# First convolution with one-hot tables laid out node number by node number, VectorE's order changed, weight loads moved ahead

## The chip, the cores and the metric

The kernel runs on one core of a Trainium2 chip. The metric is the device time of one execution in microseconds (us); the figure quoted is the median of the runs. The engines are TensorE (PE in the rows; PEld is its weight load), VectorE (DVE), ScalarE (ACT), GpSimd (POOL) and SyncE (SP). They work through their own instruction streams side by side and wait for one another on semaphores. A q behind an engine's name (DVEq, SPq) marks its instruction sequencer. "Window 300:1480" means from 300 to 1480 us after the start.

## The reference, cut to what matters

A graph with 12,500 nodes and 212,500 edges, sorted by the node that they end in. Three convolutions of one kind run first, then a layer norm, two layers of another kind and a last norm. Only the first convolution and the preparation ahead of it are touched.

```
def conv(h, W, b):
    m = jnp.concatenate([h[dst], h[src], edge_attr], axis=1) @ W + b
    return jax.ops.segment_sum(m, dst, num_segments=n_nodes)
h = jax.nn.relu(conv(x, W1, b1))
h = jax.nn.relu(conv(h, W2, b2))
return conv(h, W3, b3)
```

Since the sum over a node's edges commutes with the product by `W`, the kernel first sums the source nodes' rows and the edge attributes by node, and multiplies afterwards.

## The kernel before

**Tiling.** Edges stand in columns of 128 (one edge to a partition); 11 columns (`GC`) are a group, 8 groups (`TURN`) a turn, and 19 turns (`KT`) the whole. Groups alternate between two kinds, `KINDS = "EPEPEPEP"`. I call an E group and the P group behind it a quarter; there are 76 quarters.

- A **P** group fetches its source rows from HBM: GpSimd issues 11 indirect DMAs (`data<-h_parts,idx`, L913), two buffers deep.
- An **E** group fetches nothing. For each of its 11 columns ("steps" 0 to 10 below) a table of counts is made by matmuls, from `low_hot` (the low 7 bits of the source number as a one-hot row, the stationary operand) and `high_hot` (high bits and place): one of 66 columns into `p_end` (L1025), two of 506 into `p_count` (L1028). ScalarE casts `p_count` (L1152), and VectorE `p_end` in two halves (`evacuate_end`, L1366), into `adj`. A quarter later `adj` is the stationary operand of 98 matmuls against all node features `hs` (L1041, into `p_z`), 8 or 9 to each step, issued right behind the step's counts. ScalarE also sends `adj` to HBM for the later convolutions (L1161).

Both kinds sum the edge attributes, and P its rows too, by destination: 11 matmuls with `hot[:, par, j, :]` as the stationary operand (L928), `hot` being the one-hot table of the group's places, 11 blocks of 128 fp16 or bf16 numbers. `turn` (L935, L936) brings that sum into `p_node`, `finish` (L1326) adds it to `acc`, `scatter` (L1057) and `finish_dense` (L1378) do the same for `p_z`.

**What sets the order.** Each engine's stream is written out by hand in `conv_pass`; there is no scheduler. TensorE runs `dense` (11 steps; the E group's L928 behind step 1), then the P group's L928, then `scatter`. VectorE runs one `pair` (L1357, a `high_hot` table) to each step, with other work between pairs: `build_hot` (L1247) at steps 4 and 8, `rest_part` (L1278) at 3, 5, 7 and 9, `low_digits` (L1348, L1349, the next quarter's `low_hot`) at 9, `evacuate_end` and both `finish` at 6 and 2. TensorE's step m waits for pair m (`s_pair`) and for the cast of step m-2; pair m waits for the counts of step m-2, since `high_hot` has two buffers. `finish` and `finish_dense` read their base address from an SBUF table into a register (`value_load`; TENSOR_LOAD in the rows) where they need it.

**The preparation** (`prepare`) splits `x` into three bf16 parts (`xs`, `hs`), makes the tables (`chip.place`, `chip.lo`, `chip.code`), folds the weights of the two last layers (`WeightSteps`), and stores what later stages need. Layer 0's weights are loaded by SyncE behind the `hs` stores, layer 1's by GpSimd behind its iotas. Its last instruction is SyncE's wait for its stores (`s_kept`, `s_flags`, `s_parts`); all engines then meet, and the first convolution begins.

Of the kernel before, what the change touches and what calls it, by code (L numbers as in the profile page):

```python
# [25 lines left out]
P = 128  # L26
# [19 lines left out]
GC = 11  # L46
KINDS = "EPEPEPEP"
# [181 lines left out]
def prepare(chip, x_pad, src_cols, dst_pad, dst_cols, heads, col_ends, col_heads, firsts, slot_heads, flags, parts,  # L229
# [11 lines left out]
    with ExitStack() as ctx:  # L241
# [74 lines left out]
        def _(sp):  # L316
# [12 lines left out]
            steps[0].load(sp)  # L329
# [9 lines left out]
            for rows_of_it, tile in ((kept.ends, pna_ends), (kept.regs, pna_regs)):  # L339
                sp.dma_start(rows_of_it, tile[:, :, :]).then_inc(s_kept, 16)  # L340
            sp.dma_start(kept.quads, pna_quads[:, :]).then_inc(s_kept, 16)
            count = 48
            for layer, w in enumerate(ws):
                sp.wait_ge(steps[layer].s_done, 1)
                sp.wait_ge(steps[layer].s_one, 4)
                for rows_of_it, tile in zip(kept.weights[layer], w.tiles):
                    sp.dma_start(rows_of_it, tile.ap()).then_inc(s_kept, 16)
                    count += 16
            sp.wait_ge(s_kept, count)
# [4 lines left out]
        def _(pool):  # L354
            iota = lambda out, pattern, base, step: pool.iota(out, pattern, base=base, channel_multiplier=step,
                                                              allow_small_or_imprecise_dtypes=True)
            pool.memset(chip.ident[:, :], 0.0).then_inc(s_zero, 1)
            iota(chip.ramp[:, :], [[1, P]], 0, 0)
# [10 lines left out]
            for step in steps[1:]:  # L369
                step.load(pool)  # L370

        @block.vector
        def _(v):
# [10 lines left out]
            v.memset(chip.place[:, 0:2, :], -1.0)  # L384
            v.memset(chip.place[:, NGC + 2:, :], -1.0)
# [48 lines left out]
            in_group = chip.place[:, 2:NGC + 2, :].rearrange("p (h s) j -> p h s j", s=TURN)  # L434
# [6 lines left out]
            tables = [t[:, 1:NE + 1, :].rearrange("p (h s) j -> p h s j", s=NQ) for t in (chip.lo, chip.code)]  # L441
# [57 lines left out]
            v.tensor_copy(chip.cregs[:, 4, 1:], base[:, :])  # L499
            v.memset(chip.eregs[:, 2, 0:1], N)  # L500
# [41 lines left out]
        def _(act):  # L542
# [23 lines left out]
            for step in steps[1:]:  # L566
                step.scalar(nc, act, own)
# [99 lines left out]
def conv_pass(chip, layer, table, src_cols, ea_cols, W, bias, out_rows, counted, degree_rows=None):  # L667
# [29 lines left out]
    with ExitStack() as ctx:  # L697
# [8 lines left out]
        hot = sb("hot", [P, 2, GC, P], BF16)  # L706
        if first:
            low_hot = sb("low_hot", [P, 2, GC, P], F16)
            code = sb("code", [P, 2, GC])
            high_hot = sb("high_hot", [P, 2, BLOCKS * WIN], F16)  # L710
# [185 lines left out]
        def _(pool):  # L896
# [8 lines left out]

            further_windows_of(pool, further)
# [12 lines left out]
        def _(pe):  # L919
# [93 lines left out]
            def dense(k, q, count=True, between={}):  # L1013
                for i in range(GC):
                    m = q * GC + i
                    if count and first:
# [8 lines left out]
                        pe.matmul(p_end[:, b * (HI_B * WIN):(b + 1) * (HI_B * WIN)], low_hot[:, q % 2, i, :],  # L1025
                                  high_hot[:, m % 2, SPLIT:], start=True, stop=True)
                        for a in range(2):
                            mm = pe.matmul(p_count[:, m % 2, a, 0:BANK], low_hot[:, q % 2, i, :],  # L1028
# [211 lines left out]
        def _(v):  # L1240
# [3 lines left out]
            def build_hot(k, n):  # L1244
                places = chip.place[:, bass.ds(place_of(k, n), 1), :].rearrange("p a j -> p (a j)")
                ramp = chip.ramp16[:, :] if first else p_end[:, 0:P]
# [81 lines left out]
            def further(k, pos, m, x):  # L1328
# [6 lines left out]
                v.tensor_copy(near[:, :].unsqueeze(1), chip.place[:, bass.ds(k * TURN + (pos + 2), 1), :]).then_inc(s_near, 1)  # L1335
# [8 lines left out]
            def low_digits(k, q):  # L1344
                at = bass.ds(k * NQ + (q + 1), 1)
                gate(v)
                digits = chip.lo[:, at, :].rearrange("p a j -> p (a j)")
# [32 lines left out]
            def far_windows(k, q, m, x):  # L1380
# [6 lines left out]
                v.tensor_scalar(col(0).unsqueeze(1), chip.place[:, bass.ds(k * TURN + (POS_E[q] + 2), 1), :],  # L1387
# [4 lines left out]
                v.tensor_copy(col(5).unsqueeze(1), chip.lo[:, bass.ds(entry, 1), :])  # L1392
# [82 lines left out]
            if not first:  # L1475
                v.wait_ge(s_ramp, 1)
# [1042 lines left out]
```

## Time and profile before

| | us |
|---|---|
| median of 3 runs | 8308.83 (8302.76 to 8309.02) |
| profiled execution: its time | 8316.16 |
| profiled execution: span of the profile | 8314.4 |
| in it: preparation | 0 to 100.6 |
| first convolution, up to the end of its loop over edges | 100.6 to about 1480 |
| its matmuls over nodes | about 1480 to 1560 |
| all that follows | 1560 to 8314.4 |

Over the whole span TensorE is busy for 82%, GpSimd for 71%, VectorE for 53% and ScalarE for 28%. These are means over stages with different limits, so the prediction reads the preparation and the first convolution's loop by themselves. In that loop the granted TensorE clock is 1.00 throughout. The profiled execution is 7.3 us longer than the median.

### The profile page before, as it was taken

Reading aid. Unit: us, or ns where it says so; the run is one execution under the profiler, and the core shown is the slowest. Engines: PE = TensorE matmul, PEld = TensorE weight load, DVE = VectorE, ACT = ScalarE, POOL = GpSimd, SP = SyncE. Lnnn points to the kernel's source line nnn. Section 1 sums busy time; section 2 is a strip of 40 time slices with the busy share of each in tenths; the row PEclk is TensorE's granted clock in tenths of the full one; section 3 lists DMA queues with packets and bytes.
Section 4 is the critical chain, followed back from the end, with each engine's and each line's share of the span. In section 5 each row is a group of like instructions: output and inputs, shape, how many; then the busy total and the mean of one; then the engine's idle time right before and its main releaser. Section 6 shows DMA issues by size and latency. Waiting matters only on the chain. (4 is left out here: it accounts for less than half of the span.)

```text
span 8314.4 us, 168220 instructions
## 1 busy us (share of the span) xinstructions
PE 6837.9 (82%) x53896; PEld 5544.3 (67%) x53897; DVE 4427.7 (53%) x5884; ACT 2338.0 (28%) x3847; POOL 5877.8 (71%) x5876
## 2 busy tenths in 40 slices
PE   4999999888888799886788888788858888888885
PEld 3666666778888688885666666666656666566663
DVE  6777777522222222224566556566556656566665
ACT  3777777300000000002222222222242222222223
POOL 3888888177777677774777777777557777777773
PEclk9999999698888788987899889988878899898897
DMA  4655656377778777774222222222222222222222
GB/s 152 222 219 217 225 214 222 110 280 275 275 272 273 254 274 273 274 283 135 66 74 67 69 68 72 72 66 71 58 78 68 71 66 70 70 71 70 66 71 63
DMA packets 417038, 1226.32 MB, mean 147 GB/s; under 512 B 121988, under 2 KB 221694, under 8 KB 368304
## 3 DMA queue, kind: packets, MB, share of 16 engines
q1 hardware_dynamic: 216553, 744.06, 25.1%
q0 software_dynamic: 187232, 233.06, 12.9%
q10 hardware_dynamic: 13160, 248.08, 7.4%
q8 instruction: 44, 0.72, 0.0%
q14 instruction: 49, 0.40, 0.0%
HBM read 943.22 MB, written 281.51 MB: 147 GB/s over the span
## 5 line engine op out<-in xcount | busy, mean ns | idle before, releaser
L1913 POOL DMA_INDIRECT data<-q_rows,idx x3328 | 3163.8, 951 | 1145.3 <-issue 998.6
L913 POOL DMA_INDIRECT data<-h_parts,idx x2508 | 2676.0, 1067 | 1098.9 <-issue 1077.9
L1041 PE MATMUL p_z<-hs,adj 128*128 128x192 bf16 x22442 | 2115.6, 252 | 61.8 <-issue 61.7
L1041 PEld LDWEIGHTS p_z<-hs,adj 128*128 128x128 bf16 x22442 | 1934.2, 100 | 314.0 <-issue 106.1
L2045 ACT COPY back<-p_back 128x1024 f32<-128x1024 f32 x418 | 423.2, 1013 | 2385.1 <-PE p_back L1933 2385.1
L2115 DVE TENSOR_TENSOR_SCAN run<-reset,run,p_turn 128x1024 f32<-128x1024 bf16 x416 | 974.2, 2342 | 145.0 <-PE p_turn L1980 141.4
L1152 ACT CAST adj<-p_count 128x1012 bf16<-128x1012 f32 x836 | 918.7, 1105 | 334.6 <-PE p_count L1028 334.5
L573 DVE TENSOR_TENSOR hot<-p_ramp,ends 128x2048 f32<-128x2048 f32 x416 | 949.7, 2283 | 0.6 <-issue 0.5
L1939 PE MATMUL part<-hot,t 128*128 128x128 f32 x6688 | 908.7, 295 | 45.5 <-issue 45.5
L1939 PEld LDWEIGHTS part<-hot,t 128*128 128x128 f32 x6688 | 878.6, 212 | 46.1 <-issue 46.1
L1944 PE MATMUL part<-hot,back 128*128 128x128 f32 x6688 | 815.1, 275 | 0.0
L2082 DVE TENSOR_TENSOR t<-data,p_feat 128x512 f32<-128x512 f32 x416 | 285.7, 687 | 978.7 <-DMA data<-q_rows,idx 719.9
L1933 PEld LDWEIGHTS p_back<-ident,run 128*128 128x128 f32 x3344 | 428.4, 157 | 557.3 <-issue 557.3
L1944 PEld LDWEIGHTS part<-hot,back 128*128 128x128 f32 x6688 | 779.8, 192 | 0.0
L1933 PE MATMUL p_back<-ident,run 128*128 128x128 f32 x3344 | 511.6, 303 | 244.1 <-DVE run L2115 244.0
L1925 PE MATMUL p_feat<-w_edge_feat,feat 128*128 128x512 f32 x832 | 482.2, 664 | 208.1 <-DVE acc L2143 171.3
L1301 DVE TENSOR_REDUCE zs<-p_z 128x64 f32<-128x192 f32 x229 | 80.7, 352 | 964.9 <-PE p_z L1041 964.9
L1226 ACT CAST idx<-src_near 128x11 int32 x228 | 45.7, 201 | 1816.6 <-DMA data<-h_parts,idx 1738.3
L1028 PE MATMUL p_count<-high_hot,low_hot 128*128 128x506 f16 x1672 | 495.7, 377 | 0.0
L1357 DVE TENSOR_SCALAR high_hot<-iota,code 128x1078 f16<-128x1078 f16 x838 | 420.8, 510 | 51.7 <-PE p_count L1028 44.0
L1980 PE MATMUL p_turn<-ident,t 128*128 128x128 f32 x3328 | 435.7, 274 | 0.0
L928 PE MATMUL p_part<-data,hot 128*128 128x192 bf16 (+1 forms) x2508 | 281.9, 264 | 175.0 <-DMA data<-h_parts,idx 174.8
(314 smaller groups left out, 6388.5 us busy)
## 6 DMA issues: line engine op xcount, KB each, us to landing
adj<-counted SPq DMA_DIRECT2D x304, 1568.0 KB
counted<-adj ACTq DMA_DIRECT2D x76, 3136.0 KB
reset<-flags SPq DMA_DIRECT2D x208, 512.0 KB
data<-q_rows,idx POOLq DMA_INDIRECT x3328
data<-h_parts,idx POOLq DMA_INDIRECT x2508
feat<-in_ea_blocks SPq DMA_DIRECT2D x208, 128.0 KB
ea<-in_ea_cols SPq DMA_DIRECT2D x154, 88.0 KB, 1.9
rden<-node_rows SPq DMA_DIRECT2D x50, 256.0 KB
```

The lines of the kernel that those rows point to most:

```text
L573: return v.tensor_tensor(hot.rearrange("p t j n -> p (t j) n"), chip.p_ramp[:, :].unsqueeze(1).broadcast_to([P, 2 * G, P]), places.unsquee ...
L913: pool.indirect_dma_start(out=data[:, p % HELD, j, 0:PARTS], out_offset=None, in_=table[:, :], in_offset=bass.IndirectOffsetOnAxis(ap=idx[ ...
L1028: mm = pe.matmul(p_count[:, m % 2, a, 0:BANK], low_hot[:, q % 2, i, :], high_hot[:, m % 2, a * BANK:(a + 1) * BANK], start=True, stop=True)
L1041: mm = pe.matmul(p_z[:, 0:PARTS], adj[:, (q + LAG) % 2, hi, :], hs[:, hi, :], start=(hi == 0), stop=(hi == BLOCKS - 1))
L1152: nc.scalar.copy(to, p_count[:, m % 2, :, 0:BANK].rearrange("p a (h w) -> p a h w", w=WIN))\
L1913: pool.indirect_dma_start(out=data[:, r, j, :], out_offset=None, in_=q_rows[:, :], in_offset=bass.IndirectOffsetOnAxis(ap=idx[:, r, j:j + ...
L1925: pe.matmul(p_feat[:, r % 2, :], feat[:, r, :], w.edge[:, :, :].rearrange("p j f -> p (j f)"), start=True, stop=True).then_inc(s_feat, 1)
L1933: b = pe.transpose(p_back[:, j * P:(j + 1) * P], run[:, par, j * P:(j + 1) * P], chip.ident[:, :])
L1939: pe.matmul(part[:, x, 0, :], t3[:, slot, j, 1:3, :].rearrange("p b f -> p (b f)"), hot[:, par, 0, j, :], start=(j == 0), stop=(j == G - 1))
L1944: m = pe.matmul(part[:, x, 1, :], back[:, j, :], hot[:, par, 1, j, :], start=(j == 0), stop=(j == G - 1))
L1980: m = pe.transpose(p_turn[:, j * P:(j + 1) * P], t3[:, r, j, 0:2, :].rearrange("p b f -> p (b f)"), chip.ident[:, :])
L2115: v.tensor_tensor_scan(run[:, r % 2, :], reset[:, r, :], p_turn[:, :], run[:, (r + 1) % 2, GE - 1:GE], ALU.add, ALU.max).then_inc(s_run, 1)
```

## The change

**Tables.** In the first convolution a table is no longer 11 blocks of 128 numbers but 128 blocks of 12 (`GW`), a node number's 11 columns and one of padding side by side. The number ramp against which it is compared is written out in that form (`wide_ramp`, 1536 numbers, by GpSimd at the start of the convolution); `chip.place` and `chip.lo` get rows of 12. TensorE takes a column's table as stationary operand with 12 numbers from one element to the next.

**VectorE.** `low_digits` goes from step 9 to behind step 10. The bases of the two `finish` of a quarter come packed from one `value_load` ahead of the first pair (`both_begins`, table `chip.begins`); `finish_dense` uses the one already read, but for the first quarter of a turn.

**Preparation.** GpSimd loads both layers' weights ahead of its iotas, ScalarE makes both layers' weights before `start`, and SyncE stores them before it stores `flags` and the `kept` tables.

```diff
@@ prepare, SyncE
-            steps[0].load(sp)
             sp.wait_ge(s_wins, 1)
...
-            sp.wait_ge(s_start, 1)
-            sp.dma_start(flags.rearrange("(p e) -> p e", p=P), start[:, :]).then_inc(s_flags, 16)
-            sp.wait_ge(s_pna, 1)
...
             for layer, w in enumerate(ws):
                 sp.wait_ge(steps[layer].s_done, 1)
...
+            sp.wait_ge(s_start, 1)
+            sp.dma_start(flags.rearrange("(p e) -> p e", p=P), start[:, :]).then_inc(s_flags, 16)
+            sp.wait_ge(s_pna, 1)
...
@@ prepare, GpSimd
             pool.memset(chip.ident[:, :], 0.0).then_inc(s_zero, 1)
+            for step in steps:
+                step.load(pool)
...
-            for step in steps[1:]:
-                step.load(pool)
@@ prepare, VectorE and ScalarE
+            halves = chip.begins[:, :].bitcast(I16)
+            v.memset(halves[:, 0:1], N)
+            v.tensor_copy(halves[:, 1:NGC + 1], base[:, :])
...
-            steps[0].scalar(nc, act, own)
+            for step in steps:
+                step.scalar(nc, act, own)
             act.wait_ge(s_begin, 1)
@@ conv_pass
+            wide_ramp = sb("wide_ramp", [P, P, GW], F16)
+            wide_hot = sb("wide_hot", [P, 2, P, GW], BF16)
+            low_hot = sb("low_hot", [P, 2, P, GW], F16)
...
+            if first:
+                pool.iota(wide_ramp[:, :, :], [[1, P], [0, GW]], base=0, channel_multiplier=0,
+                          allow_small_or_imprecise_dtypes=True).then_inc(s_ramp, 1)
...
-                    mm = pe.matmul(p_part[:, columns(pos)], hot[:, par, j, :],
+                    mm = pe.matmul(p_part[:, columns(pos)], wide_hot[:, par, :, j] if first else hot[:, par, j, :],
...
-                        pe.matmul(p_end[:, b * (HI_B * WIN):(b + 1) * (HI_B * WIN)], low_hot[:, q % 2, i, :],
+                        pe.matmul(p_end[:, b * (HI_B * WIN):(b + 1) * (HI_B * WIN)], low_hot[:, q % 2, :, i],
...
+                if first:
+                    return v.tensor_tensor(wide_hot[:, n % 2], wide_ramp[:, :, :],
+                                           chip.place[:, bass.ds(place_of(k, n), 1), :].broadcast_to([P, P, GW]), ALU.is_equal)
...
-                v.tensor_tensor(low_hot[:, q % 2], chip.ramp16[:, :].unsqueeze(1).broadcast_to([P, GC, P]),
-                                digits.unsqueeze(2).broadcast_to([P, GC, P]), ALU.is_equal)
+                v.tensor_tensor(low_hot[:, q % 2], wide_ramp[:, :, :], chip.lo[:, at, :].broadcast_to([P, P, GW]),
+                                ALU.is_equal)
...
+            def both_begins(k, pos):
+
+                two = v.value_load(chip.begins[0:1, bass.ds(k * (TURN // 2) + pos // 2, 1)], min_val=0,
+                                   max_val=(N << 16) + N)
+                low = v.snap((two & 0xffff).with_bounds(min_val=0, max_val=N))
+                return low, v.snap((two >> 16).with_bounds(min_val=0, max_val=N))
...
+                    before, begins[pos] = both_begins(k, pos)
+                    for i in range(2, GC):
+                        pair(k, q, i)
...
+                        if i == GC - 1:
+                            low_digits(k, q + 1)
```

**Place A: VectorE, behind the pair of step 6.** `p_end` is the first half's counts, `cregs` the table of bases, `high_hot` at the end the pair of step 7. Before:

```order
L1366 CAST adj<-p_end 128x6x6x11
L1316 ISA
L1316 TENSOR_LOAD cregs
L1316 ISA x2
L1326 ISA
L1326 TENSOR_TENSOR acc<-acc,p_node 49x128
L1370 ISA
L1370 TENSOR_SCALAR to_window<-ramp,slots 128x128
L1357 TENSOR_SCALAR high_hot<-iota_2,code 128x1078
```

With the change:

```order
L1379 CAST adj<-p_end 128x6x6x11
L1340 ISA
L1340 TENSOR_TENSOR acc<-acc,p_node 49x128
L1383 REGISTER_ALU
L1383 TENSOR_SCALAR to_window<-ramp,slots 128x128
L1370 TENSOR_SCALAR high_hot<-iota_2,code 128x1078
```

The register load has gone from between the cast and the sum; the next pair follows with nothing else between.

**Place B: VectorE, from the pair of step 9 on.** `low_hot` is the next quarter's table; the `high_hot` rows are the pairs of steps 9 and 10 and the next quarter's 0. Before:

```order
L1357 TENSOR_SCALAR high_hot<-iota_2,code 128x1078
L1276 REGISTER_ALU
L1278 TENSOR_TENSOR dense_ea<-ea,dense_ea 128x11x16
L1348 ISA
L1348 COPY code<-code 128x11
L1349 REGISTER_ALU
L1349 TENSOR_TENSOR low_hot<-ramp_2,lo 128x1408
L1356 REGISTER_ALU
L1357 TENSOR_SCALAR high_hot<-iota_2,code 128x1078
L1356 REGISTER_ALU
L1357 TENSOR_SCALAR high_hot<-iota_2,code 128x1078
```

With the change:

```order
L1370 TENSOR_SCALAR high_hot<-iota_2,code 128x1078
L1290 REGISTER_ALU
L1292 TENSOR_TENSOR dense_ea<-ea,dense_ea 128x11x16
L1369 REGISTER_ALU
L1370 TENSOR_SCALAR high_hot<-iota_2,code 128x1078
L1361 ISA
L1361 COPY code<-code 128x11
L1362 ISA
L1362 TENSOR_TENSOR low_hot<-wide_ramp,lo 128x1536
L1369 REGISTER_ALU
L1370 TENSOR_SCALAR high_hot<-iota_2,code 128x1078
```

The pair of step 10 now stands ahead of the table, which has 1536 elements instead of 1408.

**Place C: GpSimd, start of the preparation.** `own_place` is what VectorE's first instruction on the parts of `x` stands behind (`s_place`). Before:

```order
L357 MEMSET ident 128x128
L355 ISA
L355 IOTA ramp 128x128
L355 IOTA shifts 128x100
L355 IOTA near_shifts 128x32
L355 IOTA slot_w 128x1
L355 IOTA slot_w 128x11
L355 IOTA own_place 128x8
```

With the change:

```order
L357 MEMSET ident 128x128
L171 DMA wp_3<-in_L_gnn_W_pre 64x192
...
L171 DMA wo_3<-in_L_gnn_W_post 64x3x64 x5
L355 ISA
L355 IOTA ramp 128x128
...
L355 IOTA own_place 128x8
```

Thirty DMA issues, 15 for each layer, now stand between the memset and the iotas.

## Rows read from the trace of the kernel before

**Rows 1.** Busy time by stretch: length, PE, PEld, DVE, ACT, POOL, clock, DMA, GB/s.

```profile
500.00:1000.00 500.00, 456.60 (x4440) 340.46 (x4439) 378.36 (x781) 363.20 (x475) 404.12 (x308) 1.00 0.60 219
```

**Rows 2.** Groups by line and form, window 300:1480: count, busy us, mean ns, idle before.

```profile
L913 POOL DMA_INDIRECT data<-h_parts,idx x723 | 952.4, 1317 | 225.7 <-issue 225.7
...
L1247 DVE TENSOR_TENSOR hot<-ramp,place 128x1408 bf16<-128x1408 f16 x132 | 212.6, 1610 | 0.0
...
L1349 DVE TENSOR_TENSOR low_hot<-ramp,lo 128x1408 f16<-128x1408 f16 x66 | 106.6, 1615 | 0.0
...
L1278 DVE TENSOR_TENSOR ea<-ea,data 128x176 f32<-128x176 f32 x65 | 22.3, 343 | 18.9 <-ACT data L1173 18.9
...
L936 PEld LDWEIGHTS p_node<-ident,by_place 128*113 128x113 f32 x132 | 18.2, 178 | 0.0
```

**Rows 3.** Longest wait of TensorE, window 300:1480: total us, times, longest.

```profile
PE p_end L1025 <- DVE high_hot L1357: 74.9, 99, 0.9
```

**Rows 4.** Timeline, one quarter, TensorE at steps 6 to 10: start, length, instruction.

```profile
716.29 0.19 PE L1025 MATMUL p_end<-high_hot,low_hot 128*128 128x66 f16 x1 [0.20 <-DVE adj L1366]
...
718.08 0.19 PE L1025 MATMUL p_end<-high_hot,low_hot 128*128 128x66 f16 x1 [0.43 <-ACT adj L1152]
...
719.28 0.19 PE L1025 MATMUL p_end<-high_hot,low_hot 128*128 128x66 f16 x1
...
720.69 0.19 PE L1025 MATMUL p_end<-high_hot,low_hot 128*128 128x66 f16 x1
...
722.96 0.19 PE L1025 MATMUL p_end<-high_hot,low_hot 128*128 128x66 f16 x1 [0.91 <-DVE high_hot L1357]
```

**Rows 5.** Timeline, the same quarter, VectorE.

```profile
715.47 0.57 DVE L1366 CAST adj<-p_end 128x396 bf16<-128x396 f32 x1 [0.69 <-PE p_count L1028]
...
716.92 0.28 DVE L1326 TENSOR_TENSOR acc<-acc,p_node 49x128 f32 x1 [0.88 <-issue]
...
717.44 0.50 DVE L1357 TENSOR_SCALAR high_hot<-iota,code 128x1078 f16<-128x1078 f16 x1
...
720.79 1.61 DVE L1349 TENSOR_TENSOR low_hot<-ramp,lo 128x1408 f16<-128x1408 f16 x1
...
722.32 0.90 DVE L1357 TENSOR_SCALAR high_hot<-iota,code 128x1078 f16<-128x1078 f16 x2
```

**Rows 6.** Timeline, the same quarter: two gathers, and short matmuls.

```profile
708.28 0.95 POOL L913 DMA_INDIRECT data<-h_parts,idx  x1 [0.38 <-issue]
...
709.18 0.19 PE L1025 MATMUL p_end<-high_hot,low_hot 128*128 128x66 f16 x1
...
709.21 0.59 PE L1028 MATMUL p_count<-high_hot,low_hot 128*128 128x506 f16 x2
...
710.38 0.44 PE L928 MATMUL p_part<-dense_ea,hot 128*128 128x49 bf16 x11
...
712.07 2.30 POOL L913 DMA_INDIRECT data<-h_parts,idx  x1 [0.30 <-issue]
```

**Rows 7.** Timeline of the preparation: weight issues, VectorE on `x`, SyncE's stores.

```profile
3.22 0.76 POOL L170 DMA_DIRECT2D wp<-in_L_gnn_W_pre  x1
...
8.32 3.61 POOL L170 DMA_DIRECT2D wo<-in_L_gnn_W_post  x6
...
8.43 1.49 DVE L398 TENSOR_TENSOR xs<-xs,hs 128x1280 f32<-128x1280 f32 x1 [4.93 <-ACT hs L551]
...
30.19 0.22 DVE L411 CAST identb<-ident 128x128 bf16<-128x128 f32 x1
...
70.44 0.34 SPq L340 DMA_DIRECT2D kept_ends<-pna_ends  x1
...
79.12 0.60 SPq L347 DMA_DIRECT2D kept_w<-w_beta  x1
```

**Rows 8.** DMA busy tenths and GB/s, window 60:105, 40 slices of 1.125 us.

```profile
DMA  0063000000998907999099993420000000000710
GB/s 0 7 257 121 0 15 0 0 0 0 440 364 281 350 1 266 219 11 8 0 16 16 11 22 14 35 53 0 0 0 0 0 0 0 0 0 4 169 38 4
```

More of the change, by code:

```diff
@@ L46 @@
 GC = 11
+GW = 12
 KINDS = "EPEPEPEP"
@@ L440, in _ @@
             v.wait_ge(s_src, 16)
-            tables = [t[:, 1:NE + 1, :].rearrange("p (h s) j -> p h s j", s=NQ) for t in (chip.lo, chip.code)]
+            tables = [t[:, 1:NE + 1, 0:GC].rearrange("p (h s) j -> p h s j", s=NQ) for t in (chip.lo, chip.code)]
             then(v.tensor_scalar(digit[:, 0], dense(src), 7, None, ALU.arith_shift_right))
@@ L705, in conv_pass @@
         by_place = sb("by_place", [P, KC])
-        hot = sb("hot", [P, 2, GC, P], BF16)
+        if not first:
+            hot = sb("hot", [P, 2, GC, P], BF16)
         if first:
-            low_hot = sb("low_hot", [P, 2, GC, P], F16)
+            wide_ramp = sb("wide_ramp", [P, P, GW], F16)
+            wide_hot = sb("wide_hot", [P, 2, P, GW], BF16)
+            low_hot = sb("low_hot", [P, 2, P, GW], F16)
             code = sb("code", [P, 2, GC])
@@ L1244, in build_hot @@
             def build_hot(k, n):
-                places = chip.place[:, bass.ds(place_of(k, n), 1), :].rearrange("p a j -> p (a j)")
-                ramp = chip.ramp16[:, :] if first else p_end[:, 0:P]
+                if first:
+                    return v.tensor_tensor(wide_hot[:, n % 2], wide_ramp[:, :, :],
+                                           chip.place[:, bass.ds(place_of(k, n), 1), :].broadcast_to([P, P, GW]), ALU.is_equal)
+                places = chip.place[:, bass.ds(place_of(k, n), 1), 0:GC].rearrange("p a j -> p (a j)")
+                ramp = p_end[:, 0:P]
                 return v.tensor_tensor(hot[:, n % 2], ramp.unsqueeze(1).broadcast_to([P, GC, P]),
@@ L1474, in _ @@
             v.memset(scratch[:, 27:28], 0.0).then_inc(s_by_sum, 1)
-            if not first:
-                v.wait_ge(s_ramp, 1)
+            v.wait_ge(s_ramp, 1)
             for n in range(1 if first else 2):
@@ L1488, in _, with first_turn @@
             far_turns(v, far_windows)
-            with v.Fori(0, KT) as k:
+            def both_begins(k, pos):
[3 more added lines that the diff above has]
+                return low, v.snap((two >> 16).with_bounds(min_val=0, max_val=N))
+            def first_turn(k):
+                begins = {}
@@ L1490, in _ @@
                 for pos in range(TURN):
                     if pos in POS_P:
+                        q = POS_E.index(pos - 1)
+                        dense_begin = begins[pos - 3] if pos - 3 in begins else dense_begin_of(k, q)
+                        sum_z(k, q)
+                        sum_places(k, pos)
+                        finish_dense(k, q, k * H + (nth[pos] + 1 + BEFORE), dense_begin)
+                        continue
+                    q = POS_E.index(pos)
+                    before, begins[pos] = both_begins(k, pos)
@@ new lines, in first_turn @@
+                    for i in range(2, GC):
+                        pair(k, q, i)
+                        if i == 2:
+                            finish(k, pos - 1, before)
+                        if i in (3, 5):
+                            rest_part(k, nth[pos] + 1, (i - 3) // 2)
+                        if i in (4, 8):
+                            table_free(k, nth[pos] + (1 if i == 4 else 2))
+                            build_hot(k, nth[pos] + (1 if i == 4 else 2)).then_inc(s_hot, 1)
+                        if i == 6:
+                            evacuate_end(k, q, 0)
+                        if i == 6:
+                            finish(k, pos, begins[pos])
+                            place_slots(k, q)
+                        if i in (7, 9):
+                            rest_part(k, nth[pos] + 2, (i - 7) // 2)
+                        if i == GC - 1:
+                            low_digits(k, q + 1)
@@ L1492, in _ @@
+                    for i in (0, 1):
+                        pair(k, q + 1, i)
+                    evacuate_end(k, q, 1)
+            with v.Fori(0, KT) as k:
+                if first:
+                    first_turn(k)
+                for pos in (() if first else range(TURN)):
+                    if pos in POS_P:
                         dense_begin = {q: dense_begin_of(k, q) for q in done_with(pos)}
-                        if pos == POS_P[-1] and not first:
+                        if pos == POS_P[-1]:
```

61 lines of the change are left out of this document (19 added, 42 removed).

## The prediction

> **What bounds the kernel now.** I read the stages first. The change touches the preparation (100.6 us) and the loop over edges of the first convolution (about 1345 us after its start-up); the 6750 us behind them keep their instructions. In the loop no engine is the plain bound: TensorE is busy for 457 of 500 us, GpSimd for 404, VectorE for 378, ScalarE for 363, at a granted clock of 1.00, the upper level of 2.4 GHz [rows 1]. The table of low digits is built once a quarter, 66 times in 1180 us [rows 2]: a quarter takes 17.88 us, and there are 76.
>
> Next, who makes TensorE wait. Its largest wait is for VectorE's `high_hot`: 74.9 us in 66 quarters, 1.13 us each [rows 3]. The timeline of one quarter shows where. A step that nothing disturbs takes 719.28 - 718.08 = 1.20 us [rows 4]. Step 6 to 7 takes 1.79, so 0.59 is lost; step 8 to 9 takes 1.41, 0.21 lost; step 9 to 10 takes 2.27, 1.07 lost. VectorE's rows say why [rows 5]. Ahead of step 7 the half-cast ends at 716.04, the sum after it starts only at 716.92 (0.88 us "issue", the register load), and the pair runs 717.44 to 717.94; the matmul follows at 718.08. The row there names ScalarE, but the pair is what came last. Ahead of step 10, `low_hot` runs 720.79 to 722.40 and the pair behind it starts at 722.32. Step 9's pair stands behind a `hot` table in the same way. Sum: 1.87 us a quarter. Step 6 waits for the half-cast itself, which stays.
>
> GpSimd deserves a look of its own. All its idle time between gathers is "issue", 0.31 us each [rows 2]: busy plus idle is 1178 of 1180 us. A gather takes 0.95 us when left alone and 2.30 when it meets a table [rows 6]. Eleven undisturbed ones need 11 x (0.95 + 0.31) = 13.9 us, so 4.0 us a quarter go to collisions with three tables of 1.61 us (83% of their width).
>
> **The change, part by part.**
>
> *Tables in a shorter time.* Two rows give VectorE's rate: 1408 elements in 1.610 us and 176 in 0.343 [rows 2], hence 1.03 ns an element and 0.16 us fixed. At that rate 1536 elements need 1.74 us; at two elements a cycle, since ramp, places and result are all 16 bits wide and contiguous in the inner dimension, 0.95 us. No row shows a two-input 16-bit instruction with contiguous operands, so these are both ends. I take 0.95: `high_hot`, 16-bit and contiguous, does 1078 elements in 0.50 us [rows 5], well under one per cycle's time. With it step 9 loses nothing.
>
> *Order.* `low_hot` behind step 10's pair lets that pair go 1.6 us earlier, and step 10 starts on time. The table is then wanted only after 98 matmuls' tail, the P group's 11 matmuls and the scatter, over 2 us later. What is queued behind it is the pairs 0 and 1 of the next quarter and the second half-cast. One packed register load a quarter stands where VectorE has slack, ahead of the pair of step 2; the one between the half-cast and the pair of step 7 is gone, and with it the 0.88 us. Its sum, `finish`, moves earlier with it, and nobody else is late for it. So all 1.87 us should go: 76 x 1.87 = 142 us. What is late next is step 6's half-cast, unchanged.
>
> *Weight loads with 24 bytes between elements: a cost.* Every load of `low_hot` (3 a step) and `wide_hot` (11 a group) now picks single 16-bit numbers. No row shows such a load. Near end: contiguous 16-bit loads keep pace with 49-column matmuls, 11 in 0.44 us, or (0.44 - 0.19) / 10 = 0.025 us each [rows 6]. Far end: fp32 loads of 113 columns, in pairs, 18.2 us of cover for 66 pairs at 178 ns each, follow each other after 0.276 - 0.178 = 0.098 us [rows 2], or 0.111 for 128. A load is hidden behind the matmul ahead of it. At length L what sticks out is: behind the 66-column matmul, which lasts 0.03 (709.18 to 709.21 [rows 6]), L - 0.027, eleven times; in the E group's sum L - 0.025, eleven times; behind a 192-column matmul (192 / 2.4 GHz = 0.080) L - 0.08, eleven times; behind a 242-column one L - 0.10, eleven times. With L = 0.111 that is 11 x 0.21 = 2.3 us a quarter; with 0.025 nothing. I take twice the contiguous time, 0.051, nearer the row of the same type and form: 11 x (0.024 + 0.026) = 0.55, say 0.57 us a quarter with rounding, 43 us in all.
>
> Two statements of the Trainium skill pull apart here. "TensorE: Matmul & The Clock Gate", section "Weight-path perf modes", gives fast weight load's read pattern as four chunks of 32 columns, "packed or strided"; by that alone the load stays as it is and the whole comes to 8146. "SBUF - State Buffer" (Door 1, the note on cachelines) says that reads lose their rate when each goes to another 16-byte line, as they would at 24 bytes. No run so far shows either.
>
> *GpSimd.* Its collisions shrink with the tables: 83% of 3 x 0.95 = 2.4 us, so 16.2 us a quarter, under the 16.6 forecast for TensorE. The Trainium skill ("SBUF - State Buffer", Who interferes with whom) infers that `tensor_tensor` does not hold up descriptor generation; the trace disagrees, with 2.30 us against 0.95 [rows 6].
>
> *Preparation.* GpSimd needs 8.32 + 3.61 - 3.22 = 8.7 us to issue 15 loads [rows 7]; thirty in front of the iotas end at about 18.4, so VectorE's work on `x` begins near 20 and not at 8.43. It was waiting for pieces of `x` then and will not be now: ten instructions, one each 1.45 us, bring it to 34.5, where it had been at 30.2 [rows 7]. The rest of its stream follows 4.3 us later, plus 0.5 for new small instructions, so `kept_ends` goes out at 75.2, not 70.44. Against this stands the tail. SyncE's last issue ends at 79.7 [rows 7], the next stage starts at 100.6, and DMA stays busy at 11 to 53 GB/s until about 91.5 [rows 8], with the weight stores as the last in the queue. These now go out between about 46 and 62 us, under VectorE's work (the cover; without it they cost what they cost now). The 836 KB of `kept_ends` took some 3.5 us at 280 to 440 GB/s [rows 8]: stage end near 80 instead of 100.6. Should the tail belong to whatever is stored last, 76.2 + 20.9 = 97.1. I take 19 us, ends 3.5 and 21.
>
> *Start of the convolution.* `wide_ramp` is some 1.5 us on GpSimd, beside VectorE's memsets of several us; the first gathers are wanted 30 us later. Two tables ahead of the loop save 2 x 0.66 = 1.3 us.
>
> **Sum.** 142 - 43 + 19 + 1 = 119 us. 8316.2 (the profiled execution's time) - 119 = 8197; that execution was 7.3 above the median, so 8190.
>
> **The rivals.**
>
> *The strided load is as quick as before.* For it: the same instruction form. Then 8316.2 - 7.3 - 142 - 20 = 8147; should GpSimd at 16.2 us a quarter be the bound, 76 x 1.68 = 128 us and 8161.
>
> *The tables take 1.74 us,* or GpSimd or a later wait takes over. Step 9 keeps its 0.21 and 0.13 more, and the next quarter's first steps lose some 0.3: gain 1.2 - 0.57 = 0.65 us, 49 + 20 us, 8240. Against it: all three operands meet what `high_hot` meets.
>
> *Slower: TensorE becomes bound by its weight loads.* Place: the 44 loads a quarter named above. With L = 0.111 the cost is 2.3 us against 1.87 gained: 76 x 0.41 = 31 us lost, 20 won back, 8320, no change. From L = 0.113 on it is over 0.2% slower; at 0.15 it is 11 x (0.123 + 0.125 + 0.07 + 0.05) = 4.0 us, 2.2 a quarter, 164 - 20 = 144 us, 8453. For it: four chunks are read at once, each from another place at each element. Against it: the fp32 row moves twice the bytes and still does a column in 0.87 ns.
>
> *The change does not do what it says*: the moved table and the gone register load are plain in the instruction order, so only the preparation's tail could stay (8205); it is inside the forecast.
>
> **How the numbers follow.** Forecast, L from 0.035 to 0.075: 0.38, 8190 (8160 to 8240). Quick load: 0.25, 8147 to 8161. Long tables or another bound: 0.12, 8240. L from 0.075 to 0.10: 0.07, 8240 to 8290. L from 0.10 to 0.113, no change: 0.06. Slower: 0.12. Faster 0.82, same 0.06, slower 0.12; 0.2% (17 us) is about what a measurement of this kernel can tell from no change. The range 8135 to 8300 leaves out the slower case and the upper part of no change.
>
> **What would show each step.** In the changed kernel's profile: `wide_hot` and `low_hot` at 0.95 us; steps 7, 9 and 10 at 1.20 us plus the load; the 11 matmuls of 49 columns in 0.44 us (quick), near 0.7 (forecast) or over 1.3 (slower); a quarter of 16.6 us; gathers with a mean near 1.17 us (0.95 plus 2.4 / 11); the first convolution starting near 81 us. The forecast is wrong if those 11 matmuls take over 1.3 us, if ScalarE's casts turn out to pace the steps, or if the stage start stays at 97 or later.

## The result and the profile after

| | us |
|---|---|
| before, median (same chip) | 8305.8 (8298.6 to 8309.0) |
| after, median | 8208.1 (8207.5 to 8211.6) |
| ratio | 0.988, 95% interval 0.987 to 0.990 |
| after, profiled execution (span) | 8208.1 (8206.4) |

The change takes 98 us away. 8190 was forecast, in a range of 8135 to 8300. By the barriers between the stages, in the two profiled executions: preparation 100.0 us before, 79.5 after; first convolution 1543.5 and 1471.2. The stages behind them, whose code is the same, were 15 us shorter in the later execution. About half of that is the 7 us by which the profiled execution of before lay above its median; the other 8 us have no cause that a run shows. What the change did is therefore read from the two stages alone: 20.5 + 72.3 us.

Of the changed kernel, the busy time in the stretch of [rows 1]:

```profile
500.00:1000.00 500.00, 494.37 (x4701) 407.20 (x4699) 345.32 (x827) 386.30 (x502) 329.74 (x324) 1.00 0.64 233
```

TensorE was busy for 457 of 500 us and is for 494 now: it bounds the loop. Its groups and VectorE's and GpSimd's, window 300:1380, against [rows 2]:

```profile
L924 POOL DMA_INDIRECT data<-h_parts,idx x703 | 719.7, 1024 | 363.3 <-issue 194.7 <-PE p_part L939 168.5
...
L1039 PEld LDWEIGHTS p_count<-high_hot,low_hot 128*128 128x128 f16 x1404 | 147.9, 157 | 0.0
...
L1257 DVE TENSOR_TENSOR wide_hot<-wide_ramp,place 128x1536 bf16<-128x1536 f16 x128 | 121.6, 950 | 0.0
...
L1362 DVE TENSOR_TENSOR low_hot<-wide_ramp,lo 128x1536 f16<-128x1536 f16 x63 | 60.0, 952 | 0.0
```

The tables take 0.95 us instead of 1.61. A gather takes 1.02 us in the mean instead of 1.32, and 168.5 us of GpSimd's idle time now are waits for TensorE, where all of it had been "issue". The wait of [rows 3] is gone; the only one left of its kind, same window:

```profile
PE p_end L1036 <- DVE adj L1379: 8.8, 32, 0.3
```

Against [rows 4, 6], TensorE in one quarter of the changed kernel, steps 1 and 2 and 6 to 10:

```profile
692.26 0.78 PE L939 MATMUL p_part<-dense_ea,wide_hot 128*128 128x49 bf16 x11
...
692.88 0.22 PE L1036 MATMUL p_end<-high_hot,low_hot 128*128 128x66 f16 x1
...
698.72 0.22 PE L1036 MATMUL p_end<-high_hot,low_hot 128*128 128x66 f16 x1 [0.21 <-DVE adj L1379]
...
699.98 0.19 PE L1036 MATMUL p_end<-high_hot,low_hot 128*128 128x66 f16 x1
...
701.21 0.19 PE L1036 MATMUL p_end<-high_hot,low_hot 128*128 128x66 f16 x1
...
702.45 0.19 PE L1036 MATMUL p_end<-high_hot,low_hot 128*128 128x66 f16 x1
...
703.68 0.19 PE L1036 MATMUL p_end<-high_hot,low_hot 128*128 128x66 f16 x1
```

Step 7 follows 1.26 us after step 6, where it had been 1.79; step 9 after 1.24 (1.41) and step 10 after 1.23 (2.27). But the undisturbed step was 1.20 and is 1.24, and eleven 49-column matmuls take 0.78 us where they took 0.44: they start 0.059 us apart, not 0.026. Two amounts of opposite sign, then, and the experiments are there to part them. The clearest view is the mean time from a step's first matmul to the next step's, worked out from all quarters between 300 and 1250 us of each trace that have no record missing. The column names the step that it begins with, 10 holds the P group too, and the last one is the mean length of a quarter in the same stretch. Labels are those of the experiments below.

| kernel | 0 | 1 | 2 | 3 | 4 | 5 | 6 | 7 | 8 | 9 | 10 | quarter |
|---|---|---|---|---|---|---|---|---|---|---|---|---|
| before | 1.36 | 1.49 | 1.20 | 1.20 | 1.65 | 1.54 | 1.79 | 1.20 | 1.41 | 2.27 | 2.81 | 17.91 |
| after | 1.44 | 1.86 | 1.26 | 1.23 | 1.68 | 1.65 | 1.26 | 1.24 | 1.24 | 1.23 | 2.85 | 16.94 |
| e1, old tables | 1.51 | 1.49 | 1.20 | 1.20 | 1.65 | 1.54 | 1.20 | 1.20 | 1.23 | 1.20 | 3.83 | 17.25 |
| e2, new tables alone | 1.44 | 1.87 | 1.26 | 1.23 | 1.68 | 1.61 | 1.43 | 1.26 | 1.23 | 1.34 | 2.88 | 17.24 |
| e6, short tables, packed | 1.36 | 1.49 | 1.20 | 1.20 | 1.65 | 1.54 | 1.20 | 1.20 | 1.20 | 1.20 | 2.82 | 16.04 |
| e7, low digits at step 9 | 1.44 | 1.87 | 1.26 | 1.23 | 1.68 | 1.65 | 1.26 | 1.23 | 1.24 | 1.36 | 2.88 | 17.10 |
| e8, loads apart | 1.44 | 1.87 | 1.26 | 1.23 | 1.68 | 1.61 | 1.43 | 1.26 | 1.24 | 1.23 | 2.85 | 17.10 |

### The profile page after: what moved, and what is told of

Read it like the earlier page. It is cut to its first block and busy times, and to the rows that moved or that the text cites. A ratio compares the mean times of both kernels' runs of the same rounds, so it can differ in the third digit from the quotient of the medians.

```text
span 8206.4 us, 167771 instructions
## 1 busy us (share of the span) xinstructions
PE 6866.8 (84%) x53896; PEld 5674.2 (69%) x53897; DVE 4283.2 (52%) x5889; ACT 2343.2 (29%) x3847; POOL 5635.0 (69%) x5892
## 5 line engine op out<-in xcount | busy, mean ns | idle before, releaser
L924 POOL DMA_INDIRECT data<-h_parts,idx x2508 | 2433.9, 970 | 1174.3 <-issue 963.4
L1039 PE MATMUL p_count<-high_hot,low_hot 128*128 128x506 f16 x1672 | 524.3, 396 | 0.0
L2067 ACT ACTIVATE t<-t 128x512 f32<-128x512 f32 x416 | 262.8, 632 | 560.0 <-DVE t L2113 558.7
```

Source lines behind the costliest of these rows:

```text
L924: pool.indirect_dma_start(out=data[:, p % HELD, j, 0:PARTS], out_offset=None, in_=table[:, :], in_offset=bass.IndirectOffsetOnAxis(ap=idx[ ...
```

## The experiments

The two theories at the start. **A**: the gain is the waits that went, less what TensorE pays for operands 24 bytes apart; TensorE bounds the loop, so packed operands would be faster still. **B**: the shorter tables bring the gain (over VectorE, or over GpSimd, which they no longer hold up), and the loads do not matter.

**e1, the old tables back.** All 11 blocks of 128 and the old compare, the rest as in after:

```diff
-mm = pe.matmul(p_part[:, columns(pos)], wide_hot[:, par, :, j] if first else hot[:, par, j, :],
+mm = pe.matmul(p_part[:, columns(pos)], hot[:, par, j, :],
-v.tensor_tensor(low_hot[:, q % 2], wide_ramp[:, :, :], chip.lo[:, at, :].broadcast_to([P, P, GW]),
+v.tensor_tensor(low_hot[:, q % 2], chip.ramp16[:, :].unsqueeze(1).broadcast_to([P, GC, P]),
```

> The changed kernel with the one-hot tables of the kernel before: 11 blocks of 128 elements, written one element a cycle (1.61 us each), and stationary operands that lie packed. VectorE's new order and the new preparation stay. Theory A (TensorE bounds the changed loop, and what it pays for the strided operands, 0.85 us a quarter, is more than what VectorE's 0.66 us a table saves): the quarter falls from 16.94 to about 16.5 us, the first convolution by about 35 us, the whole to about 8175 us, and the 49-column matmuls stand 0.026 us apart again instead of 0.058. Theory B (the faster tables are what brought the gain; the order alone moves waits about): TensorE waits for VectorE's column compares again, the quarter goes to 17.4 us or more, the whole to 8240 us or more.

Measured: 8241.6 us, ratio to before 0.992 (0.990 to 0.994), 28 us slower than after by the ratios. A missed the time by some 65 us. B's time (8240 or more) was met, but by luck: the engine that it named is not the one that TensorE waits for. Its waits and its gathers, window 300:1380:

```profile
POOL data L918 <- issue: 209.4, 687, 0.3
...
PE p_part L933 <- DMA data<-h_parts,idx: 39.6, 16, 2.5
```
```profile
L918 POOL DMA_INDIRECT data<-h_parts,idx x690 | 871.3, 1263 | 210.3 <-issue 209.4 <-PE p_part L933 0.9
```

Steps 0 to 9 are as good as they get (table above): the order alone takes all of VectorE's lateness away, long tables or not. The loss sits in the last column, where about once a turn TensorE waits 2.5 us for gathered rows. GpSimd needs 11 x (1.26 + 0.30) = 17.2 us a quarter and is idle for nothing but "issue". The first three turns of the loop still run at 16.34 us a quarter; then its lead is used up and the waits begin. Behind 12 of the 16 waits the granted clock is 0.50 for a stretch (columns as in [rows 1]):

```profile
431.50:434.80 3.30, 3.30 (x17) 1.91 (x15) 0.86 (x4) 0.68 (x1) 2.67 (x3) 0.50 0.94 380
```

so such a wait costs more than its own length. GpSimd had been just behind VectorE all the time, and the long tables keep it slow. A gather with no table beside it takes 0.95 to 0.97 us in all kernels; one that overlaps a table by over 0.05 us takes 2.30 in before and 1.74 in e1 (old tables), 1.47 in e2 and 1.12 in after (new ones), 1.27 in e6.

**e2, the new tables alone,** in the kernel before (the diff's tables, `wide_ramp` and 12 columns, nothing else of it):

> The kernel before with the new tables alone (12 columns side by side, a ramp written out so); VectorE's order, its loads of registers, and the preparation as before. Theory A: three tables a quarter are 0.66 us shorter each, which takes about 1 us of the waits out of a quarter, and the strided operands cost 0.85 us: the quarter stays within 0.2 us of 17.9, the whole at 8290 to 8310 us (ratio to before 0.998 to 1.001). Theory B: the whole falls by 60 us or more, to 8245 us or less.

Measured: 8259.3 us, 0.993 (0.992 to 0.995): 53 us gained, between the two. The tables alone remove most of the same waits that the order removes, so the parts do not add up: order alone 0.66 us a quarter, tables alone 0.67 (their cost to the loads included), both 0.97. What the new order adds to the new tables is 0.30 us, in columns 6 and 9, which e8 and e7 undo one by one.

**e3, the preparation alone,** in the kernel before (weight loads, ScalarE's steps and SyncE's stores as in after):

> The kernel before with the change of the preparation alone: both layers' weight loads ahead of GpSimd's iotas, ScalarE's weight steps ahead of the start flags, the weights stored ahead of the rest. Theory A (the preparation's end hung on the stores of the weights, and the loop gains nothing from this): the preparation ends at 79.5 us instead of 100.0, all other stages stay, the whole falls by 20 us to about 8286 us. Rival: the cost of the earlier loads comes back in the first convolution, whose loop starts at another moment relative to its transfers: the gain is under 12 us.

Measured: 8295.1 us, 0.998 (0.997 to 0.999), 18 us; the stage ends at 79.4 us by the barriers, the first convolution takes 1543.2 against 1543.5. The theory holds; nothing comes back in the first convolution.

**e4, packed and short: four copies of each number.** If both a quick load and a short table are wanted, the compare must read runs of 16-bit numbers without the table being turned. VectorE first copies each column's number four times side by side, one step ahead of each table:

```diff
+v.tensor_copy(four_p[:, n % 2, :, :], chip.place[..., 0:GC]...unsqueeze(2).broadcast_to([P, GC, CP])).then_inc(s_four, 1)
+v.wait_ge(s_four, ...)
+v.tensor_tensor(hot[:, n % 2].rearrange("p j (n c) -> p j n c", c=CP), <ramp16 in fours>, <four_p, broadcast over n>, ALU.is_equal)
```

> A new form: the tables are 11 packed blocks of 128 as before, but each column's number is first copied four times side by side by VectorE (44 elements, one step ahead), so that the compare reads and writes runs of four 16-bit elements on all three operands. VectorE's new order and the new preparation stay. Theory A with two elements a cycle for such runs: a table takes about 0.9 us, the packed operands load quickly, the quarter is 15.9 to 16.3 us and the whole 8130 to 8160 us. If runs of four are not enough for two elements a cycle, a table takes 1.6 us and the whole is that of the first kernel of this set plus up to 15 us for the copies (8175 to 8195 us). Theory B (TensorE's loads do not matter): the whole stays at 8208 us within 10.

Measured: 8331.4 us, 1.002 (1.001 to 1.003), slower than before: the largest miss of the set. The tables did take 0.88 us. The timeline of VectorE behind a branch to the loop's top, and a DMA queue of window 250:1380 (packets, MB, share), say what went wrong:

```profile
411.07 0.50 DVE L1382 TENSOR_SCALAR high_hot<-iota,code 128x1078 f16<-128x1078 f16 x1 [9.55 <-issue]
```
```profile
q14 instruction: 78, 0.64, 0.2%
```

VectorE stands still for 8.5 us behind the branch, every turn, and a queue of instructions moves data in the loop that moves none in those of before, after and e1 to e3. TensorE then has nothing to do, and behind this stop its granted clock is 0.50 (columns as in [rows 1]):

```profile
407.60:414.30 6.70, 2.58 (x14) 1.91 (x15) 2.82 (x7) 1.44 (x2) 5.04 (x6) 0.50 0.45 133
```

The granted clock of 500:1000 is 0.94 in the mean. The Trainium skill ("Runtime: NRT & Kernel Launch", Instruction fetch mechanics) says that most engines hold a window of two blocks of 256 instructions, and that a taken branch to a place outside it waits for a fetch. VectorE's loop has 285 instructions here, and as many in before.

**e5, the same, 32 instructions further on:**

```diff
+for _ in range(32 if first else 0):
+    v.memset(pad[:, _:_ + 1], 0.0)
 with v.Fori(0, KT) as k:
```

> The form with four copies again, unchanged but for 32 one-element memsets that VectorE runs once, ahead of the first convolution's loop. The run before this one spent 8.5 us at VectorE's branch back to the loop's top in every turn, with packets on an instruction queue that no other kernel shows there. Theory (the loop of 285 instructions of VectorE lies across one boundary more of its instruction memory than it does in the kernel before, where it has 285 too but begins a few instructions earlier): moved on by 32 instructions the loop no longer does, the instruction packets and the 8.5 us go, a turn takes 66 us and the whole 8175 to 8195 us. Rival (the waits on the new semaphore, or the four-fold copies themselves, stop VectorE there): nothing changes, 8325 to 8340 us.

Measured: 8156.2 us, 0.981 (0.980 to 0.983). 32 useless instructions make the kernel 175 us faster; the loop has no packet on that queue any more, and a turn takes 64.17 us instead of 74.04. The theory holds, the rival falls. The time is 19 us below what was expected: a standstill costs 9.9 us a turn, more than its own 8.5 us, since TensorE's clock is at the lower level behind it.

**e11, the kernel before, ten instructions further on.** The same edit with 10 in place of 32:

> The kernel before with ten one-element memsets of VectorE ahead of the first convolution's loop, run once: the loop of 285 instructions then begins 838 instructions into VectorE's program instead of 828. With the new tables alone it began at 831, with the loads apart at 834, both undisturbed; with three copies a quarter it began at 835 and was stopped, at 867 it was not. Theory (the place of the loop decides): instruction packets and some 8 us at every branch back, 19 turns, the whole at 8450 to 8480 us. Rival (something else in the form with copies stopped it): 8300 to 8320 us.

Measured (one execution): 8442.6 us against 8310.3, 132 us slower; 8.3 us behind nearly every branch (7.6 at two), and in the loop:

```profile
q14 instruction: 60, 0.49, 0.1%
```

That is 7 us below the range expected, with the mechanism as expected. The place of the loop decides: begun 828, 831 or 834 instructions into VectorE's program (before, e2, e8) it runs undisturbed, at 835 and 838 (e4, e11) it is stopped, at 867 (e5) it is not. (VectorE's records in the traces give the same distances from before: 3, 6, 7, 10 and 39.) By the rule of the Trainium skill quoted above, an estimate: 28 of every 256 starts would make a loop of 285 reach into a third block, and only 4 would do so for one of 261, the changed kernel's. The runs agree as far as they go, since 28 starts from 835 to 862 fit all six. This is a fit: with blocks of 256 counted from the same zero as the starts, the 28 would be 740 to 767 and 996 to 1023, so the runs show neither where a block begins nor that the width is 28.

**e6, the copies once a turn,** two instructions (352 and 176 elements) at step 3 of a turn's first quarter; the loop has 258:

```diff
+v.tensor_copy(four_p[:, :, :, :], chip.place[:, bass.ds(k * TURN + 3, TURN), 0:GC].unsqueeze(3).broadcast_to([P, TURN, GC, CP]))
+v.tensor_copy(four_lo[:, :, :, :], chip.lo[:, bass.ds(k * NQ + 2, NQ), 0:GC].unsqueeze(3).broadcast_to([P, NQ, GC, CP]))
```

> The form with four copies, the copies made once a turn (8 columns groups of node places, 4 of low digits, two instructions) instead of three times a quarter: VectorE's loop has 258 instructions. Tables stay 0.88 us, operands packed. Theory A (TensorE bounds the loop of the changed kernel and the strided operands cost it 0.85 us a quarter): the quarter is 16.1 to 16.5 us, the whole 8140 to 8175 us, faster than the changed kernel's 8208 us; the 49-column matmuls stand 0.026 us apart. Theory B (strided operands cost nothing that counts, GpSimd or ScalarE bounds the loop at 16.9 us): 8200 to 8215 us.

Measured: 8148.4 us, 0.980 (0.979 to 0.982): faster than both kernels, by 166 and (from the ratios) 69 us. Busy time in 500:1000, and the rows of window 300:1250 for the tables and loads:

```profile
500.00:1000.00 500.00, 494.92 (x4966) 383.56 (x4964) 358.14 (x889) 405.73 (x531) 366.17 (x344) 1.00 0.67 246
```
```profile
L1260 DVE TENSOR_TENSOR hot<-ramp,four_p 128x1408 bf16<-128x1408 f16 x119 | 104.3, 877 | 0.0
...
L1037 PEld LDWEIGHTS p_count<-high_hot,low_hot 128*128 128x128 f16 x1304 | 82.8, 98 | 0.7
```

TensorE is as busy as in after and gets 5.6% more done. This settles A: the difference to after, 0.90 us a quarter, lies nearly all between matmuls that load the strided operand (the split is given below); the tables are 0.07 us shorter too, but TensorE hardly waits for them in either kernel. B's bound at 16.9 us does not exist.

**e7 and e8, two parts of VectorE's new order undone,** each by itself in after:

```diff
-                        if i == GC - 1:
+                        if i == 9:
                             low_digits(k, q + 1)
```
```diff
-                    before, begins[pos] = both_begins(k, pos)
-                            finish(k, pos - 1, before)
+                            finish(k, pos - 1)
-                            finish(k, pos, begins[pos])
+                            finish(k, pos)
```

> The changed kernel with one step of VectorE's order undone: the table of low digits is written at step 9 again instead of step 10. Theory A (TensorE bounds the loop, VectorE has slack at step 9 with 0.95 us tables): at most 0.1 us a quarter, 8205 to 8218 us. Rival (the place matters still, since ScalarE's casts and the column compares at steps 9 and 10 are late): TensorE's wait for high_hot comes back with 0.3 us a quarter or more, 8230 us or more.

> The changed kernel with another step undone: VectorE loads the node number of each window by itself again, instead of two from one word; its loop is back at 285 instructions. Theory A (TensorE bounds the loop): at most 0.15 us a quarter, 8205 to 8222 us. Rival (a register load holds VectorE's queue for 0.3 to 0.4 us, and that comes through to TensorE): 0.3 us a quarter, 8230 us. Third case: its loop begins within one instruction of the one that was stopped for 8.5 us a turn, and is stopped so too: 8350 us with packets on the instruction queue.

Measured: 8231.5 us, 0.990 (0.989 to 0.992), and 8231.3 us, 0.990 (0.988 to 0.992). The kernel before ran 8 us slower on that occasion than beside after, so by the ratios they lose 15 and 14 us, by the quarters 0.15 and 0.16 us (12 us). Both medians lie above A's ranges as written and at the rivals' times. By the ratios, e8 is at A's upper edge and e7 5 us above it; by the quarter, e8 is at A's limit of 0.15 and e7 over its 0.1, and both are at half of the rivals' 0.3. So A holds roughly for the loads and was too low for the move. Undoing the move costs 0.13 us in column 9 and undoing the packed load 0.17 in column 6, where before had lost 1.07 and 0.59. With tables of 0.95 us the one is worth an eighth of that, the other three tenths.

**e9, the load by itself.** After, with eight sets of 16 matmuls of 49 columns ahead of the convolution's work, the stationary operand with 1, 2, 3, 4, 6, 8, 12 and again 1 element from one to the next:

> The changed kernel with a probe ahead of TensorE's work in the first convolution: eight sets of 16 matmuls of 49 columns, whose 128x128 16-bit stationary operand is read from one tile with 1, 2, 3, 4, 6, 8, 12 and again 1 elements from one to the next (2 to 24 bytes). At 1 the matmuls should stand 0.026 us apart, at 12 0.058 to 0.061, as they do in the loops. Theory A (the quick load needs packed elements): every step from 2 on costs 0.059. Theory B (the load reads memory in pieces of some bytes, and pays for each piece that it opens): 0.026 to 0.03 at 2, growing with the step to 0.059 at 8 or 12. The time of the whole says nothing here, up to 15 us over 8208.

The windows are those of the sets, in order (PE and PEld busy; a count includes the three to five that reach in from the set ahead):

```profile
82.24:82.91 0.67, 0.66 (x16) 0.67 (x17) 1.00 0.19 41
82.91:83.58 0.67, 0.67 (x21) 0.67 (x19) 1.00 0.08 18
83.58:84.24 0.66, 0.66 (x21) 0.66 (x19) 1.00 0.04 7
84.24:84.91 0.67, 0.67 (x21) 0.67 (x19) 1.00 0.05 12
84.91:85.64 0.73, 0.73 (x21) 0.73 (x19) 1.00 0.00 0
85.64:86.64 1.00, 1.00 (x20) 1.00 (x19) 1.00 0.03 8
86.64:87.64 1.00, 1.00 (x19) 1.00 (x19) 1.00 0.28 66
87.64:88.04 0.40, 0.40 (x19) 0.40 (x18) 1.00 0.33 69
```

The second set at step 1 takes 0.40 us, 0.025 each, the first one 0.67, 0.042 each, and 49 columns at 1.2 GHz are 0.041: TensorE had stood idle for 28 us and ran at the lower level at first. The 1.00 printed there is no reading, for the trace has no clock record ahead of 85.16 us, in the fifth set. So the first four sets show only that a load with 2, 3 or 4 elements between (4 to 8 bytes) takes no more than 0.042 us; A's form of it (0.059 at every step but 1) falls. At 6 elements (12 bytes) it is 0.047, at 8 and 12 (16 and 24 bytes) 0.062, the same for both; the second half of the set at 12 has 0.060, near the loops' 0.059. That answers to reads in pieces of 16 bytes, as the note in "SBUF - State Buffer" (Door 1) of the Trainium skill has it. At 12 bytes three of four elements lie in another piece than the one before, at 16 and 24 every one does, and 0.047 is three quarters of 0.062; pieces of 8 or 32 bytes would not give these three numbers. That the Trainium skill calls the read pattern "packed or strided" ("TensorE: Matmul & The Clock Gate", Weight-path perf modes) is no sign that the step costs nothing: from 6 elements on it costs. What steps of 2 to 4 cost at 2.4 GHz stays open.

**e10, e6 with GpSimd's iotas ahead of the 30 weight loads:**

> The form with four copies made once a turn, and in the preparation GpSimd's iotas ahead of both layers' 30 weight loads instead of behind them. In the changed kernel VectorE waits 16.2 us for GpSimd's own_place, issued behind those loads, and its chain ends with the stores of the node ends at 75.4 us and the stage at 79.5. Theory (VectorE's chain ends the preparation now): it starts at 8.4 us, as in the kernel before, its last stores are issued at about 70.5 us, the stage ends at 74 to 76 us, the whole at 8143 us within 5. Rival (the weights' chain comes behind by as much): the stage ends at 79 us or later, 8148 us within 4.

Measured: 8146.4 us, 0.980 (0.979 to 0.982), no different from e6. It lies in both ranges expected and decides nothing. In after VectorE had waited:

```profile
19.40 1.43 DVE L394 TENSOR_SCALAR above<-own_place 128x8 f32<-128x8 f32 x1 [16.16 <-POOL own_place L355]
```

Here this instruction runs at 3.16 us and `kept_ends` goes out at 71.07 instead of 75.40, near what was expected. The stage ends at 77.9, between the theory's 74 to 76 and the rival's 79, only 1.6 us earlier than in after: the 27 packets of that store that start between 72 and 74 us take 1.45 us in the mean, where those of after (112 between 76 and 78 us) take 0.26. Why is open.

**e12, e6 with SyncE's order of stores as before:**

> The form with four copies made once a turn, and in the preparation SyncE's order of stores as before: flags, node ends and registers ahead of the two layers' weights. GpSimd's and ScalarE's new orders stay. Theory (the weights' stores take over 20 us to land, so that their place in the queue is all of the 20 us gained): they are issued behind 76 us and the stage ends at 100 to 105 us, the whole at 8168 to 8175 us. Rival (the loads and steps of the second layer ahead of the rest bring it): the stage ends at 80 to 90 us.

Measured (one execution): 8170.1 us, the stage ends at 104.8 us:

```profile
75.44 0.34 SPq L341 DMA_DIRECT2D kept_ends<-pna_ends  x1
...
84.11 0.60 SPq L348 DMA_DIRECT2D kept_w<-w_beta  x1
```

The stage ends 20 us after the last weight store is issued, as in before. The place of these stores in the queue is the whole gain of the preparation, and more (25 us here); without it the other moves of the preparation cost 5.

## Why the prediction was right, and where it was not

- **What bounds.** Right: no plain bound before, VectorE late at steps 7, 9 and 10. e6 is the kernel with nothing but these waits taken away, and its quarter is 17.91 - 16.04 = 1.87 us shorter, the very sum read from [rows 4, 5].
- **Tables in 0.95 us.** Right, 0.950 and 0.952 measured; 1.74 is out.
- **Waits gone, 142 us.** Right as a sum. The reasons given to its parts were less exclusive than told: e1 and e2 show that the order alone or the tables alone removes most of it. The text gave the order all but the 0.21 us of step 8, and did not see that without short tables GpSimd stops the loop at 17.2 us (e1). Its own rows had the warning, with GpSimd busy or between two issues for 1178 of 1180 us. That makes the short tables necessary, for GpSimd's sake.
- **Weight loads, 43 us: the mis-sized term.** L was taken as 0.051 and is 0.059 in the loop. By kind of neighbours, after less e6, a quarter: within the E group's sum 0.31 us (forecast 0.29), between a 66-column matmul and the first 506-column one 0.15 (forecast 0.26), and between the two 506-column ones 0.35 (forecast nothing). The overlap is what the prediction had wrong: it held the load behind the first 506-column matmul to be hidden, and it costs 0.032 each time. The rest, 0.09, is spread over the other places. In all 0.90 us, 68 us instead of 43. Why a load behind 0.21 us of matmul is not hidden is not shown by any run.
- **GpSimd, 16.2 us a quarter.** Wrong in size, right in its consequence. A gather takes 1.02 us in the mean, not 1.17: one that meets a table of the new form takes 1.12, and the collisions cost 11 x (1.02 - 0.95) = 0.8 us a quarter, not 2.4. GpSimd's need is 11 x 1.33 = 14.6 us.
- **Preparation, 19 us.** Right at 20.5. `kept_ends` goes out at 75.40 (forecast 75.2), the first convolution starts at 80.2 (forecast near 81). Of the two owners of the tail it was the weight stores (e12).
- **The sum.** 142 - 43 + 19 + 1 = 119 us forecast; 142 - 68 + 20.5 gives 94.5, and measured are 93 us in the two stages and 98 in the medians. In the two stages the gain is 26 us short of the forecast, and this one term accounts for 25 of it. That the forecast of the whole was only 18 us too low is partly luck: the unchanged stages were 8 us shorter for no known reason.
- **Rivals.** "As quick as before" is out in this layout, and e6 reaches its 8147 by another way (8148). "Slower by loads" had the mechanism, at half of the L that it needed. "Another bound takes over" is e1, not after.

## What to carry to other kernels

When two engines are close behind the one that is waited for, shorten or move one thing alone and see which of them appears: here the waits for VectorE hid a GpSimd that was only 0.7 us a quarter better off (17.2 against 17.9). A table has a writer and a reader; turned for the writer's sake it cost the reader half of the gain, while repeating the small operand in runs of four served both. In a rolled loop look at the idle time behind the branch and at the instruction queue among the DMA queues, before an edit is judged by where it happened to put the loop.

## What the runs showed that I had not expected

- **The place of a loop in the instruction stream:** mostly 8.3 to 8.5 us (7.5 to 7.6 at some) behind each branch when a loop of 285 instructions of VectorE begins 835 or 838 instructions into its program, nothing at 828, 831, 834 and 867; 132 to 175 us on the whole.
- **Quick compares with runs of four:** a compare of 1408 16-bit elements whose operands are contiguous only in fours takes 0.88 us, and 1.61 in the old form. Less the fixed 0.16 us that the prediction worked out, that is twice the rate.
- **A strided stationary operand:** 0.025 us packed, 0.047 at 12 bytes, 0.062 at 16 and 24 bytes (0.059 in the loops) from one 16-bit element to the next.
- **Collisions of gathers with tables** cost 4.0 us a quarter in before and 0.8 in after, while the tables' own time only fell from 4.83 to 2.85: their form counts, and where they lie, not only their length.
- **A granted clock of 1.00 that is no reading.** Ahead of the trace's first clock record (85.16 us in e9) the profile prints 1.00, while the first four sets, behind 28 us of idleness, run at half rate (0.042 us for 49 columns, 0.025 in the last set).
- **A stop of another engine costs TensorE more than its length,** since its clock is at the lower level behind it: 9.9 us a turn for 8.5 us in e4.
